# A two-layer decoder on one core: two attention stages with their products in another order

## The reference, cut to what matters

```python
# block 1, channel attention: the scores are channel by channel, 256 x 256
q, k, v = xn @ Wq, xn @ Wk, xn @ Wv                 # xn = layernorm(x)
w = softmax(einsum('bse,bsf->bef', q, k) / sqrt(8))
x = x + einsum('bef,bsf->bse', w, v) @ Wo

# block 4, linear attention: 16 heads of 16, chunks of 128 tokens
q, k = rotate(silu(xn @ Wq)), rotate(silu(xn @ Wk)); v = xn @ Wv
o = ((q @ k^T) * decay_mask) @ v                    # one chunk: no carried state
gate = xn @ Wg1 @ Wg2                               # Wg1: 256 x 16, Wg2: 16 x 256
o = group_rmsnorm(o * sigmoid(gate)) * norm_weight
x = x + o @ Wo
```

## Time and profile before

| | us |
|---|---|
| median of 3 runs | 1319.75 (1319.05 to 1320.85) |
| the profiled execution | 1320.28 |
| its span, first to last instruction | 1318.3 |
| PE busy in the span | 1182.8 (90%) |
| DVE busy | 774.4 (59%) |
| ACT busy | 580.5 (44%) |
| POOL busy | 603.9 (46%) |

### The profile page before, as it was taken

The page is one execution under the profiler, slowest core; times in us unless marked ns, Lnnn a source line. Parts: engine busy times, 40 slices in busy tenths (PEclk is TensorE's granted clock), DMA queues, the critical chain, the costliest instruction groups (busy, mean ns, idle before and its releaser), DMA issues. The chain is left out here.

```text
span 1318.3 us, 24667 instructions
## 1 busy us (share of the span) xinstructions
PE 1182.8 (90%) x7421; PEld 831.5 (63%) x7422; DVE 774.4 (59%) x1930; ACT 580.5 (44%) x1504; POOL 603.9 (46%) x752
## 2 busy tenths in 40 slices
PE   7997889967989869978999999999999759999995
PEld 5774556544555534446888888888888536666663
DVE  4553688865887749955667767767666422222221
ACT  3432676643333300016656766666676323333331
POOL 2001465533655537636556666656665112232322
PEclk9998999988999979979999999999999869999998
DMA  7000000002998030041000000000002212222323
GB/s 259 0 0 12 14 18 12 13 1 81 187 206 170 1 154 12 0 188 72 5 13 13 13 15 15 20 12 12 12 17 77 85 43 42 47 44 44 47 41 88
DMA packets 46354, 69.41 MB, mean 53 GB/s; under 512 B 4736, under 2 KB 42672, under 8 KB 45232
## 3 DMA queue, kind: packets, MB, share of 16 engines
q1 hardware_dynamic: 37136, 52.95, 15.1%
q0 software_dynamic: 7152, 9.34, 4.4%
q10 hardware_dynamic: 2000, 6.29, 1.3%
HBM read 57.12 MB, written 32.58 MB: 68 GB/s over the span
## 5 line engine op out<-in xcount | busy, mean ns | idle before, releaser
L1742 PE MATMUL ga.pkq<-ga.xnT,g.early 128*128 128x128 f32 x1280 | 157.0, 276 | 1.0 <-ACT ga.halves L1660 1.0
L1742 PEld LDWEIGHTS ga.pkq<-ga.xnT,g.early 128*128 128x128 f32 x1280 | 151.6, 193 | 9.6 <-issue 8.2
L1522 POOL TENSOR_TENSOR ga.halves<-ga.halves,g.ga_sinT 128x512 f32<-128x512 f32 x80 | 103.3, 1291 | 51.6 <-ACT ga.halves L1660 51.6
L1786 PE MATMUL ga.turn_out<-g.early,ga.aT 128*128 128x256 f32 x512 | 118.3, 385 | 0.3 <-ACT ga.aT L1682 0.3
L1667 ACT ACTIVATE ga.e<-ga.psc,ga.negmax 128x128 f32<-128x128 f32 x256 | 90.6, 366 | 46.9 <-DVE ga.negmax L1588 45.9
L1530 POOL TENSOR_TENSOR ga.kqT<-ga.by_cos,ga.halves 128x512 f32<-128x512 f32 x80 | 102.6, 1283 | 16.5 <-issue 16.5
L1786 PEld LDWEIGHTS ga.turn_out<-g.early,ga.aT 128*128 128x128 f32 x512 | 95.9, 192 | 12.7 <-ACT ga.aT L1682 0.7
L1897 DVE TENSOR_TENSOR ex.hidden<-ex.silu,ex.p 128x512 f32<-128x512 f32 x39 | 26.8, 687 | 124.3 <-PE ex.p L1950 117.9
L1575 DVE TENSOR_TENSOR ga.by_cos<-ga.pkq,g.ga_cosT 128x512 f32<-128x512 f32 x80 | 55.3, 691 | 72.5 <-PE ga.pkq L1742 44.6
L1767 PE MATMUL ga.paT<-ga.pT,ga.v 128*128 128x512 f32 x128 | 68.4, 617 | 12.3 <-ACT ga.pT L1675 9.1
L1945 PE MATMUL ex.p<-g.spare,ex.xnT 128*128 x156 | 76.9, 616 | 1.1 <-ACT ex.xnT L1925 0.8
(11 more groups left out here) (290 smaller groups left out, 2630.2 us busy)
## 6 DMA issues: line engine op xcount, KB each, us to landing
mo_rows<-in_pad_rows SPq DMA_DIRECT2D x1, 18447.0 KB, 101.4
ex.row<-mo_rows SPq DMA_DIRECT2D x39, 129.0 KB, 2.1
g.spare<-in_mo_w SPq DMA_DIRECT2D x1, 4096.0 KB, 12.1
g.late<-in_mo_w SPq DMA_DIRECT2D x1, 4096.0 KB, 22.7
g.early<-in_mo_w SPq DMA_DIRECT2D x1, 4096.0 KB, 12.4
g.ctxT<-in_ctxR SPq DMA_DIRECT2D x1, 2048.0 KB, 11.9
xa.ctxT<-in_ctxT SPq DMA_DIRECT2D x16, 128.0 KB, 2.5
g.spare<-cv_rows SPq DMA_DIRECT2D x1, 2048.0 KB, 8.0
```

Of the source, the lines that this page charges most:

```text
L1522: nc.gpsimd.tensor_tensor(by_sin[:, par, :].rearrange("p (h t) -> p h t", h=REP), halves[:, par, :].rearrange("p (h t) -> p h t", h=REP), ...
L1742: last = nc.tensor.matmul(pkq[:, par, j * P:(j + 1) * P], w[:, q, at * P:(at + 1) * P], xnT[:, s.par, q, :], start=(q == 0), stop=(q == C ...
L1786: last = nc.tensor.matmul(pout, aT[:, h // REP, (h % REP) * P:(h % REP + 1) * P], g.ga_wo[:, h, :], start=(h == 0), stop=(h == H - 1))
```

## The change

In channel attention, `w` is turned on PE by four transposes into a new PSUM tile `pwT`, copied by DVE to `wT`, and multiplied with v one step later (`pmix`, now 128 output columns); ACT divides by the softmax sums while it copies (`mixed`, two instructions), and the output product takes `ca_wo` as it was loaded. DVE no longer scales `wo`, and copies `vT` earlier in its step. In linear attention, `la_wg1` times `la_wg2` is multiplied out once at the stage's start and kept beside `la_wv`; v and gate then come from one product with 512 columns, into `pvx`. The narrow product, its copy `g1T` and the second gate product go. `xn` is turned one batch ahead, k is turned into `pvx`, and on PE `po` of b comes before the turn of `un` of a; `pout` of a moves behind the turn of `oT` of b and to the tile `turn`. ACT copies `oT` before `unT`. The SP queue issues as many DMAs as before, with `la_wg1` loaded turned. DVE's and POOL's loops in linear attention keep their lines.

```diff
-    g.la_wv, at = cut(at, C, D)
+    g.la_wvg, at = cut(at, C, 2 * D)
...
-    g.la_wg1, at = cut(at, C, 16)
+    g.la_wg1T, at = early[0:16, at:at + D], at + D
...
                     dve.wait_ge(w_ready, upto(b))
-                    nc.vector.reciprocal(rowsum[:, b.par, :], rowsum[:, b.par, :])
-                    dve.drain()
-                    if b.base is None and b.n == 0:
-                        dve.wait_ge(g.ca_o_loaded, 16)
+                    nc.vector.reciprocal(rowsum[:, b.par, :], rowsum[:, b.par, :]).then_inc(sum_ready, 1)
+                if s.on:
+                    dve.wait_ge(vT_done, upto(s))
+                    if s.past(2):
+                        dve.wait_ge(mix_done, upto(s, back=2))
+                    nc.vector.tensor_copy(vT[:, s.par, :, :], pv[:, 0:D]).then_inc(vT_ready, 1)
+                b = s.back(1)
+                if b.on:
+                    dve.wait_ge(w_turned, upto(b))
                     if b.past(2):
                         dve.wait_ge(mix_done, upto(b, back=2))
-                    for c in range(C):
-                        last = nc.vector.tensor_scalar(wo[:, b.par, c, :], g.ca_wo[:, c, :], rowsum[:, b.par, c:c + 1],
-                                                       None, ALU.mult)
-                    last.then_inc(wo_ready, 1)
+                    nc.vector.tensor_copy(wT[:, b.par, :, :], pwT[:]).then_inc(wT_ready, 1)
...
-                if s.on:
-                    dve.wait_ge(vT_done, upto(s))
-                    if s.past(2):
-                        dve.wait_ge(out_done, upto(s, back=2))
-                    nc.vector.tensor_copy(vT[:, s.par, :, :], pv[:, 0:D]).then_inc(vT_ready, 1)
...
+                b = s.back(2)
+                if b.on:
+                    act.wait_ge(mix_done, upto(b))
+                    act.wait_ge(sum_ready, upto(b))
+                    if b.past(2):
+                        act.wait_ge(out_done, upto(b, back=2))
+                    for c in range(C):
+                        last = nc.scalar.activation(mixed[:, b.par, c, :], pmix[:, c * P:(c + 1) * P], ACT.Copy,
+                                                    scale=rowsum[:, b.par, c:c + 1])
+                    last.then_inc(mix_ready, 1)
...
-                        act.wait_ge(mix_done, upto(b, back=2))
+                        act.wait_ge(w_turned, upto(b, back=2))
+                        act.wait_ge(mix_ready, upto(b, back=2))
...
-                if b.on:
-                    act.wait_ge(mix_done, upto(b))
-                    if b.past(2):
-                        act.wait_ge(out_done, upto(b, back=2))
-                    nc.scalar.activation(mix[:, b.par, :, :], pmix[:], ACT.Copy).then_inc(mix_ready, 1)
...
                     last.then_inc(scores_done, 1)
                 b = s.back(2)
                 if b.on:
-                    pe.wait_ge(mix_ready, upto(b))
+                    pe.wait_ge(wT_ready, upto(b))
                     pe.wait_ge(vT_ready, upto(b))
                     if b.past(1):
-                        pe.wait_ge(x_added, upto(b, back=1))
+                        pe.wait_ge(mix_ready, upto(b, back=1))
                     for c in range(C):
-                        last = nc.tensor.matmul(pout[:, 0:D], vT[:, b.par, c, :], mix[:, b.par, c, :],
-                                                start=(c == 0), stop=(c == C - 1))
-                    last.then_inc(out_done, 1)
+                        for f in range(C):
+                            last = nc.tensor.matmul(pmix[:, c * P:(c + 1) * P], wT[:, b.par, f, c * P:(c + 1) * P],
+                                                    vT[:, b.par, f, :], start=(f == 0), stop=(f == C - 1))
+                    last.then_inc(mix_done, 1)
...
                     last.then_inc(qk_done, 1)
+                b = s.back(2)
+                if b.on:
+                    pe.wait_ge(mix_ready, upto(b))
+                    if b.base is None and b.n == 0:
+                        pe.wait_ge(g.ca_o_loaded, 16)
+                    if b.past(1):
+                        pe.wait_ge(x_added, upto(b, back=1))
+                    for c in range(C):
+                        last = nc.tensor.matmul(pout[:, 0:D], mixed[:, b.par, c, :], g.ca_wo[:, c, :],
+                                                start=(c == 0), stop=(c == C - 1))
+                    last.then_inc(out_done, 1)
+                if s.on:
...
                 if b.on:
-                    pe.wait_ge(wo_ready, upto(b))
+                    pe.wait_ge(w_ready, upto(b))
                     if b.past(1):
-                        pe.wait_ge(mix_ready, upto(b, back=1))
+                        pe.wait_ge(wT_ready, upto(b, back=1))
                     for f in range(C):
                         for c in range(C):
-                            last = nc.tensor.matmul(pmix[:, f, :], w[:, b.par, c, f * P:(f + 1) * P], wo[:, b.par, c, :],
-                                                    start=(c == 0), stop=(c == C - 1))
-                    last.then_inc(mix_done, 1)
+                            last = nc.tensor.transpose(pwT[:, f, c * P:(c + 1) * P], w[:, b.par, c, f * P:(f + 1) * P], g.ident[:])
+                    last.then_inc(w_turned, 1)
...
-        pv, pout = pvx[:, 0:D], pvx[:, D:2 * D]
+        pv, pgate, pout = pvx[:, 0:D], pvx[:, D:2 * D], turn[:, D:2 * D]
         po, px2 = turn2[:, 0, :, :], turn2[:, 1, :, :].rearrange("p c n -> p (c n)")
-        pun, pon = pqk[:, 0:D], pqk[:, D:2 * D]
...
+        pun, pon = pvx[:, 0:D], pqk[:, D:2 * D]
...
+            act.wait_ge(wg_done, 1)
+            nc.scalar.activation(g.la_wvg[:, :, D:2 * D], pvx[:].rearrange("p (c n) -> p c n", c=C), ACT.Copy).then_inc(wg_ready, 1)
...
+                a, b, c, n1 = s.back(2), s.back(1), s.back(3), s.back(-1)
...
                 if b.on:
                     act.wait_ge(qk_turned, upto(b))
-                    act.wait_ge(qT_ready, upto(b))
                     if b.past(2):
                         act.wait_ge(scores_done, upto(b, back=2))
-                    nc.scalar.activation(kT[:, b.par, :, :], turn2[:, 1, :, :], ACT.Copy).then_inc(kT_ready, 1)
+                    nc.scalar.activation(kT[:, b.par, :, :], pvx[:, 0:D], ACT.Copy).then_inc(kT_ready, 1)
...
-                    act.wait_ge(g1_done, upto(s))
-                    if s.past(1):
-                        act.wait_ge(gate_done, upto(s, back=1))
-                    nc.scalar.activation(g1T[:], turn[0:16, D:D + P], ACT.Copy).then_inc(g1_ready, 1)
                     act.wait_ge(v_done, upto(s))
                     if s.past(2):
                         act.wait_ge(av_done, upto(s, back=2))
@@ -1012,46 +1019,51 @@
...
+                if n1.on:
+                    act.wait_ge(turned, upto(n1))
+                    if n1.past(2):
+                        act.wait_ge(v_done, upto(n1, back=2))
+                    nc.scalar.activation(xnT[:, n1.par, :, :], turn[:, 0:D], ACT.Copy).then_inc(xnT_ready, 1)
+                if b.on:
+                    act.wait_ge(av_done, upto(b))
+                    if b.past(1):
+                        act.wait_ge(o_turned, upto(b, back=1))
+                    nc.scalar.activation(oT[:], po, ACT.Copy).then_inc(oT_ready, 1)
                 if a.on:
                     act.wait_ge(un_turned, upto(a))
                     if a.past(1):
                         act.wait_ge(out_done, upto(a, back=1))
                     nc.scalar.activation(unT[:], pun, ACT.Copy).then_inc(unT_ready, 1)
-                if b.on:
-                    act.wait_ge(av_done, upto(b))
-                    if b.past(1):
-                        act.wait_ge(o_turned, upto(b, back=1))
-                    nc.scalar.activation(oT[:], po, ACT.Copy).then_inc(oT_ready, 1)
...
         @block.tensor
         def _(pe):
             pe.wait_ge(g.la_loaded, 16 * g.la_loads)
...
-                if s.on:
-                    pe.wait_ge(xn_ready, upto(s))
-                    if s.past(1):
-                        pe.wait_ge(gate_ready, upto(s, back=1))
-                    for k in range(C):
-                        last = nc.tensor.transpose(turn[:, k * P:(k + 1) * P], xn[:, s.par, k * P:(k + 1) * P], g.ident[:])
-                    last.then_inc(turned, 1)
+                a, b, c, n1 = s.back(2), s.back(1), s.back(3), s.back(-1)
                 if b.on:
                     pe.wait_ge(qk_ready, upto(b))
+                    pe.wait_ge(v_ready, upto(b))
+                    pe.wait_ge(gate_ready, upto(b))
+                    if c.on:
+                        pe.wait_ge(unT_ready, upto(c))
                     if b.past(1):
                         pe.wait_ge(oT_ready, upto(b, back=1))
                     if s.past(4):
                         pe.wait_ge(qT2_ready, upto(s, back=4))
-                    for t in range(2):
-                        for k in range(C):
```

(68 more changed lines are left out.)

35 lines of the change are left out of this document (15 added, 20 removed).

## The result

| | before | after |
|---|---|---|
| median, us | 1319.78 (1319.05 to 1324.1, 6 runs) | 1308.01 (1305.47 to 1309.83, 6 runs) |
| profiled execution | 1320.28, span 1318.3 | 1307.5, span 1305.7 |

What follows compares the result with a forecast made beforehand. PE's work alone was taken to bound channel attention, a ring through PE and DVE linear attention. Terms of -5.7 and -4.4 make -10.1 on 1320.28: 1310.2, with the median 0.5 lower, 1309.7; range 1304.5 to 1314.5.

Steps and rivals of the forecast that it cites:

- the early clock: Linear attention's start: PE works 2 us sooner, clock rises as much sooner, first q and k gain 0.9; bounds -1.1 and 0.
- PE's sum of 5.89: Channel attention's step as PE's work alone: 6.29 less 0.84 for `pmix` plus 0.44 for four transposes.
- thin hand-off of `wT`: Channel attention: `wT` ready about 0.1 us before PE wants it, so 6.00 a step was taken, not 5.89.
- lost in the first steps and kept: Channel attention's 13 steps: 0.9 us lost to other things in the first steps was expected to remain.
- Two rules: Channel attention's four added transposes: rows say 0.44 us, step 5.89; the skill's page says 0.22, step 5.67; rows were chosen.
- the ring: Linear attention's step, q and k through `a_mat`, `po`, `pout`, add and `u`: 9.65 us from 9.87, -2.8 over 13 steps.
- the wait for `un` goes: Linear attention: `un` ready about P + 5.8, under `po`, so PE's wait of 0.69 us a step vanishes.
- The fill: Linear attention's start: multiplying out the gate weights takes 1.9 us at half clock, mostly in idle time: +0.2.
- The ring at 9.87: First rival, linear attention: its step stays at 9.87 us, total 1312.5; chance 16%.
- `wT` late: Second rival, channel attention: `wT` comes late, 6.25 a step, 13 steps save 0.5, total 1313.0; chance 9%.
- a falling clock in the two stages: Fourth rival: PE falls to 1.2 GHz inside both changed stages; three such steps end at 1327.4; chance 5%.
- the third: Third rival: both changed stages run at their sums and the clock comes early, -15, total 1304.7; chance 7%.

Runs made afterwards that it cites:

- run 9: Changed kernel with DVE's copy `wT` moved behind the next batch's statistics in channel attention: 1318.19 us, step 6.666.
- run 7: Changed kernel with each of the four transposes of `w` in channel attention issued twice: 1313.62 us, step 6.348.
- run 6: Kernel before, with only linear attention's gate weights multiplied out once and the gate made in the old second product's place: 1315.11 us, step 9.375.
- run 4: Changed kernel with the old order in linear attention: turn of `un`, `po`, `pout`, turn of `oT`; ACT `unT` before `oT`: 1303.45 us, step 9.443.
- run 12: Changed kernel with only `pout` put back ahead of the turn of `oT`, `po` still first: 1307.34 us, step 9.650.
- run 2: Kernel before with only linear attention changed, channel attention as before: 1315.4 us, step 9.624.
- run 3: Changed kernel with DVE making `u` ahead of the add of `pout` in linear attention: 1299.58 us, step 9.165.
- run 5: Changed kernel with both edits, `u` ahead of the add and the old order on PE and ACT: 1304.58 us, step 9.294.
- run 10: On top of run 3, `xn2` moved from ahead of `a_mat` to between `u` and the add, turned one step later: 1297.41 us, step 9.162.
- run 11: Changed kernel with the turn of `un` put back ahead of `po` and `unT` ahead of `oT`, `pout` still last: 1315.76 us, step 10.181.
- run 8: Changed kernel with unread identity matmuls added at the head of PE's queue, six in cross attention and four in linear attention: 1307.45 us.
- run 1: Kernel before with only channel attention changed, linear attention as before: 1311.19 us, step 5.932.

## Why the prediction was right, and where its sizes were off

The total was forecast at 10.1 less and came at 11.8, and the way to it was right in both stages. That it came so near is in part luck: channel attention's steps gave 1.8 more than forecast and cross attention 2.1 that the sum has no term for, while the early clock gave 0.65 less and channel attention's start took 0.6.

**Channel attention, the step.** PE's sum of 5.89 was the step: 5.92 in the one shown, and the settled steps go 5.89 and 5.92 in turn. I took 6.00 for a thin hand-off of `wT`. The slack was thin (run 9) and yet held; 13 x 0.095 = 1.2 of the miss is here. The rest, 0.6, is "lost in the first steps and kept". In before step 2 took 7.10 and step 3 6.46, with a wait for the scaled `wo`:

```profile
22.33 1.99 PE L454 MATMUL ca.pmix<-ca.wo,ca.w 128*128 128x256 f32 x8 [0.55 <-DVE ca.wo L351]
```

The change takes that scaling out, and with it most of the loss: after's step 2 took 6.23, and under 0.4 of the 0.9 was left. The mis-sized terms are these two, together 1.8 of the 5.6. `mixed` was ready at T + 2.92 (forecast 2.9), output at T + 3.73 (3.70). The start came 0.5 late, behind a DMA of the weights.

**The transposes.** Two rules were weighed. Rows: the four turns take 0.44 and four more 0.415, where four matmuls of the same 128 columns take 0.89 (67.83 to 68.72): a transpose is twice as fast, as the row of before had it. The Trainium skill (TensorE: Matmul & The Clock Gate, Terms) has four times for fp32; the measurement decides against it here. And with turns at 1.09 of 6.35 us (run 7; 0.66 of 5.93 in after) the granted clock read 1.00. The Trainium skill (TensorE: Matmul & The Clock Gate, Part 4: PE-mode transpose) says that transposes don't count as activity the way matmuls do; at these shares of transposes the clock and the step show nothing of it.

**Linear attention, the ring.** With P at 357.69: scores P + 1.88 (forecast 1.89), `a_mat` 3.10 (3.10), `po` 5.54 (5.53), turn of `un` 6.55 (6.55), `unT` done 7.40 (7.40), `pout` 7.46 (7.45 to 7.54). From `pout` to the next q and k it is 9.65 - 7.46 = 2.19 in the mean (forecast 2.1 to 2.17). The step is 9.65, the number taken, and the wait for `u` is there, 0.61 in the step shown and 0.55 in the mean. The mechanism "the narrow product leaves the way to the scores" is shown by run 6. What I said in favour of the order, that the wait for `un` goes, is true and worth less than nothing: runs 4 and 12 show that it only moved behind `po` as a wait for `unT`. I had the turn of `un` and its copy in the chain and did not ask what the old order would give with the earlier scores; an estimate from the rows of before, with `un`, `po` and `pout` 0.54 earlier and 2.17 behind `pout`, gives 9.33, less than the 9.65 of the new order.

**Its ends.** The fill cost 0.1 (0.2). The early clock was the weakest term: -0.25 where -0.9 was forecast. The first q and k took 3.53 for 3.78. Ten of the traces have the same PE queue ahead of this group (after and runs 2 to 5, 7, 9 to 12): five took 3.78, as before did, and the others 3.65, 3.54, 3.53, 3.19 and 3.18. Run 8 put still more work ahead and got 3.78. So work 2 us sooner did not bring the clock 2 us sooner; in half of the traces it brought nothing, and even the 0.25 is a single draw. The Trainium skill (TensorE: Matmul & The Clock Gate, Part 1) says that how much of a kernel's start runs at the slow clock differs between runs of one kernel; no two traces here are of one kernel, but the ten from 3.18 to 3.78 with one queue ahead fit it. Step 1 to 2 gave 0.54 (0.4), the drain 0.33 (0.5).

**Not forecast: cross attention.** The prediction's sum has no term for it. Its code is unchanged and it took 2.1 less. Its first 30 us, before:

```profile
117.27:147.27 30.00, 23.62 (x146) 15.14 (x146) 12.97 (x34) 11.54 (x17) 9.56 (x29) 0.74 0.03 10
```

and with the old channel attention and the new linear one (run 2):

```profile
117.96:147.96 30.00, 24.38 (x142) 15.10 (x143) 12.34 (x33) 11.00 (x17) 8.92 (x27) 0.67 0.04 11
```

In the three traces with the old channel attention (before, runs 2 and 6) the clock over this stretch is 0.67 to 0.74 and the stage takes 182.0 to 183.1; in the eleven with the new one 0.83 to 0.94 and 177.4 to 180.6. So it goes with channel attention's version. It isn't the time at which the stage starts: in runs 7 and 9 it starts at 117.59 and 120.19, as late as with the old version (117.27 to 120.84), and the clock reads 0.89 and 0.83. In stretches of 5 us the clock reads 0.50, 0.63, 0.72, 0.94, 0.74, 0.92 in before, which reached 2.4 GHz and fell back; in after it reads 0.50, 0.55 and then 1.00 four times; in run 3 0.66, 1.00, 0.66 and then 1.00, so that one rose sooner and fell back once too. The clock of these 30 us isn't all of it either: at 0.84 after took 179.90 and run 1 178.84. Why the earlier stage decides this is open: I have one trace of each kernel, those of runs 2 and 6 are of the slowest execution of theirs, and no run changes the hand-over alone.

**The rivals.** The ring at 9.87, `wT` late and a falling clock in the two stages are out by the steps and by PEclk 1.00. Of the third, channel attention at its sum came true, the early clock and a linear step below 9.65 did not.

## What to carry to other kernels

Whether one queue order is better than another depends on which copy between two engines it leaves with nothing to hide under: here the same swap cost 0.21 a step or saved 0.53, by the place of a third group. So lay out the chain with the old order and the new time of its input before crediting the order. When a wait vanishes, look at the head of the next engine's queue: `u` behind an add it didn't need cost more (0.485 a step) than the change of the stage brought (0.215). A small product that stands alone ahead of the chain's head is the first thing to fold away.

## What the hardware showed

A stage's first work can run at half clock with work put ahead of it: 3.78 us for the first q and k with PE at work for 4.7 of the 5.1 us before it (run 8). An unchanged stage took 178.0 to 183.1 us, with a clock of 0.89 and 0.67 in its first 30 us (runs 3 and 2, one trace each). A 128x128 transpose in fp32 takes 0.11 us in PE's queue, half of a matmul of 128 columns (0.22). POOL's power on 128 x 16 elements takes 2.91 us and, by the traces of runs 3 and 10, is in the ring that holds linear attention's step at 9.16 once `u` is ahead of the add.
